# The weighted sum of an eight-head graph attention in three stretches in place of four, with the copy of its result a slot earlier

## Chip, cores, metric

One of the cores of a Trainium2 chip runs the whole kernel. The metric is the device time of one execution in microseconds (us), the median of several runs.

## What is computed

A stack of four graph layers over 8 batches of 1024 nodes with 64 features, each behind a layer norm and a ReLU, with a residual sum. The change concerns the fourth layer, an attention over the graph with 8 heads, followed by an attention with one head:

```
def gat_layer(x, graph, W, b):
    h = x @ W
    s = jnp.einsum('bnd,bmd->bnm', h, h) * graph
    s = jnp.where(s == 0.0, NEG_INF, s)
    a = jax.nn.softmax(s, axis=2)
    return jnp.einsum('bnm,bmd->bnd', a, h) + b
heads = jax.vmap(lambda W, b: gat_layer(flow_x, graph, W, b))(Wh, bh)
```

with 8 heads of 128 hidden features. A leaky ReLU and the second, single-head layer follow. The last sum of a head, weights times values, is what the change regroups.

## The kernel before, in words

`hidden_attention` (from line 335) does the 8 heads. A *unit* g is one head of one batch; there are 64, eight per batch. A unit has eight tiles of 128 rows by 1024 columns of scores. The scores are taken as x (W W^T) x^T, so a unit first needs y = (W W^T) x^T (`project`, L450 and L453), rounded and split into a high and a low part.

A tile goes through these steps:

- `score` (TensorE, L466): eight matmul records of 128x512 in two halves go into one of two PSUM buffers, `ps_score[i % 2]`. It waits until the mask of tile i-2 has read that buffer (`masked_ready`).
- `mask_tile` (VectorE, L559): mask and row minimum into a ring of four buffers in SBUF (the trace calls it x_sb). It waits for the scores.
- `exp_tile` (ScalarE, L627): the exponential in place, with the row sum.
- `turn_tile` (VectorE, L569): a transpose of 32x32 blocks into `weights_t`.

In the trace each score group has four matmuls (hi, lo, hi, lo) and one mask.

When all eight tiles of a unit are turned, `values` (TensorE, L484) computes the weighted sum: 32 key blocks of 32 rows, for each four matmuls, one for each group of 32 rows of the array, 256 columns wide, into four banks of `ps_low`. The trace shows eight records for a block. The 32 blocks are cut into four parts of 8 blocks, 64 records each. Then `copy_z` (ScalarE, L635) copies the sum z to SBUF, POOL divides it by the row sums (`normalise`, L694), `head_out` (TensorE, L496) multiplies it by the head's weights, `activate` (ScalarE, L642) adds the bias, `leaky` (VectorE, L574) is the leaky ReLU, and `project_out` (TensorE, L504) multiplies by wo. `take_out` (ScalarE, L651 or L654) copies the share and POOL adds it up (L705).

The order of each engine is written out by hand: a loop over g from 0 to 65, and in it over eight slots t. TensorE in slot t of unit g issues the scores of tile 8g+t+2; in slot 0 also `head_out(g-2)`; in slots 2 to 5 the four parts of `values(g-1)`; in slot 6 `project_out(g-2)`, which waits for `z_ready` of the sum just taken, since it writes one of its banks; in slot 7 `project(g+2)`. VectorE in slot t turns tile 8g+t-1 and masks tile 8g+t+2; in slot 1 it also inverts the row sums (L580), in slot 2 it does `leaky`. ScalarE in slot t does the exponential of tile 8g+t; in slot 0 also `copy_y` (L622) and `activate`, in slot 6 `copy_z` and `take_out`, in slot 7 `round_y` (L617). Part 0 of `values` waits for the last transpose of its unit and for `hidden_read`, which `activate` gives. Work queued behind a wait on the same engine waits too.

In the first two units of seven of the eight turns over the batches (g % 8 of 1 or 2, g under 56) the next batch's rows are transposed: `turn_rows` (TensorE, L443, 16 records, slot 6, behind `z_ready`), `round_rows` (ScalarE, L610), `split_rows` (VectorE, L551, slot 7), and the next `head_out` waits for that split (`x_split`).

SP stores the inverse row sums (L423) and loads them spread over the partitions (L427), and after g % 8 of 1 loads the next batch's rows in 16 transfers.

Of the kernel before, what the change touches and what calls it, by code (L numbers as in the profile page):

```python
# [334 lines left out]
def hidden_attention(nc, m, w, x_saved):  # L335

    name = "hid"
    UNITS = B * HEADS
    TILES = UNITS * NT
    Q = 32  # L340
    NB = N // Q
    RING = 4

    with ExitStack() as ctx:
# [52 lines left out]
        def wide(lo):  # L397
            return m.ps_low[:, lo:lo + 2, :].rearrange("p a n -> p (a n)")

        def y_banks(g):  # L400
            return 0 if g == 0 else 2

        def prep_bank(n, k):
            return k if n == 0 else 1
# [32 lines left out]
        def _(pe):  # L437
            def turn_rows(n, part):
                bank = prep_bank(n, part)
                for k in range(4):  # L440
                    t = 4 * part + k
                    for c in range(2):
                        ins = pe.matmul(m.ps_low[c * F:(c + 1) * F, bank, k * P:(k + 1) * P],  # L443
                                        m.h[:, t, n, :], m.ident[:], start=True, stop=True)
                ins.then_inc(x_turned, 1)
# [12 lines left out]
            def score(i):  # L458
                g, t = i // NT, i % NT
                if t == 0:  # L460
                    pe.wait_ge(y_split, g + 1)
                if i >= 2:
                    pe.wait_ge(masked_ready, i - 1)
                for half in range(2):
                    for k in range(2):
                        ins = pe.matmul(m.ps_score[:, i % 2, half * HALF:(half + 1) * HALF],  # L466
                                        xs[:, g // HEADS % 2, t * P:(t + 1) * P],
                                        y[g % 2][k][:, half * HALF:(half + 1) * HALF],
                                        start=(k == 0), stop=(k == 1))
                ins.then_inc(scores_ready, 1)  # L470

            def values(g, part):
                if part == 0:
                    if g % HEADS == 0:
                        pe.wait_ge(rows_loaded, 16 * 16 * (g // HEADS + 1))
                    pe.wait_ge(tile_turned, (g + 1) * NT)
                    if g:
                        pe.wait_ge(hidden_read, g)
                    if g + 2 < UNITS:
                        pe.wait_ge(y_copied, g + 3)  # L480
                for b in range(part * NB // 4, (part + 1) * NB // 4):
                    c = b % 2
                    for a in range(P // Q):
                        ins = pe.matmul(m.ps_low[c * F:(c + 1) * F, a, 0:NT * Q],  # L484
                                        x_rep[a * Q:(a + 1) * Q, g // HEADS % 2, b, :],
                                        weights_t[a * Q:(a + 1) * Q, g % 2, b, :, :],
                                        start=(b == c), stop=(b == NB - 2 + c))
                if part == 3:
                    ins.then_inc(values_ready, 1)

            def head_out(g):
                pe.wait_ge(z_normed, g + 1)
                if g:
                    pe.wait_ge(out_taken, g)
                for half in range(2):
                    ins = pe.matmul(m.ps_low[:, half, :], wz[:, g % HEADS, :],  # L496
                                    z[:, half * HALF:(half + 1) * HALF], start=True, stop=True)
                ins.then_inc(hidden_ready, 1)
# [24 lines left out]
            for g in range(UNITS + 2):  # L523
                n, u = g // HEADS + 1, g % HEADS
                for t in range(NT):
                    if g * NT + t + 2 < TILES:
                        score(g * NT + t + 2)
                    if t == 0 and g >= 2:
                        if n < B and u in (2, 3):
                            pe.wait_ge(x_split, 2 * n + u - 1)  # L530
                        head_out(g - 2)
                    if 2 <= t < 6 and 1 <= g <= UNITS:
                        values(g - 1, t - 2)
                    if t == 6 and n < B and u in (1, 2):
                        pe.wait_ge(z_ready, g)
                        turn_rows(n, u - 1)
                    if t == 6 and g >= 2:
                        project_out(g - 2)
                    if t == 7 and g + 2 < UNITS:
                        if g:  # L540
                            pe.wait_ge(z_ready, g)
                        else:
                            pe.wait_ge(y_copied, 2)
                        project(g + 2)
# [61 lines left out]
        @block.scalar  # L606
        def _(act):
            def round_rows(n, part):
                act.wait_ge(x_turned, 2 * n + part + 1)
                act.copy(xs[:, n % 2, part * HALF:(part + 1) * HALF],  # L610
                         m.ps_low[:, prep_bank(n, part), :]).then_inc(x_hi_ready, 1)

            def round_y(g):
                act.wait_ge(y_ready, g + 1)
                if g >= 2:
                    act.wait_ge(scores_ready, (g - 1) * NT)
                act.copy(y[g % 2][0][:], wide(y_banks(g))).then_inc(y_hi, 1)  # L617

            def copy_y(g):
                if g:  # L620
                    act.wait_ge(y_split, g)
                act.copy(y_wide[:], wide(y_banks(g))).then_inc(y_copied, 1)  # L622

            def exp_tile(i):
                g, t = i // NT, i % NT
                act.wait_ge(masked_ready, i + 1)
                act.activation(ring[:, i % RING, :], ring[:, i % RING, :], ACT.Exp, scale=-1.0,  # L627
                               bias=neg_max[:, g % 2, t:t + 1],
                               accum_out=row_sum[:, g % 2, t:t + 1]).then_inc(exp_ready, 1)

            def copy_z(g):
                act.wait_ge(values_ready, g + 1)
                if g:
                    act.wait_ge(hidden_ready, g)
                act.copy(z[:].rearrange("p (t a j) -> p a t j", t=NT, a=P // Q),  # L635
                         m.ps_low[:, :, 0:NT * Q].rearrange("p a (t j) -> p a t j", j=Q)).then_inc(z_ready, 1)

            def activate(g):
                act.wait_ge(hidden_ready, g + 1)
                if g:  # L640
                    act.wait_ge(out_ready, g)
                act.activation(hidden[:], wide(0), ACT.Identity, bias=bias[:, g % HEADS:g % HEADS + 1])\  # L642
                   .then_inc(hidden_read, 1)

            def take_out(g):
                act.wait_ge(out_ready, g + 1)
                adds = g - (g + HEADS - 1) // HEADS
                if adds > 0:
                    act.wait_ge(out_added, adds)
                if g % HEADS == 0:  # L650
                    act.copy(m.h[:, :, g // HEADS, :], m.ps_low[:, 0, :].rearrange("p (t f) -> p t f", f=F))\  # L651
                        .then_inc(out_taken, 1)
                else:
                    act.copy(share[:], m.ps_low[:, 0, :]).then_inc(out_taken, 1)  # L654

            round_rows(0, 0)
            round_rows(0, 1)
            for h in range(HEADS):
                act.wait_ge(gram_ready, h + 1)
                act.copy(gram[0][:, h, :], m.ps_low[:, h % 2, 0:P]).then_inc(gram_hi, 1)  # L660
            round_y(0)
            copy_y(0)
            round_y(1)
            for g in range(UNITS + 2):
                n, u = g // HEADS + 1, g % HEADS
                for t in range(NT):
                    if g < UNITS:
                        exp_tile(g * NT + t)
                    if t == 0 and g + 1 < UNITS:
                        copy_y(g + 1)  # L670
                    if t == 0 and g >= 2:
                        activate(g - 2)
                    if t == 6 and 1 <= g <= UNITS:
                        copy_z(g - 1)
                    if t == 6 and g >= 2:
                        take_out(g - 2)
                    if t == 6 and n < B and u in (1, 2):
                        round_rows(n, u - 1)
                    if t == 7 and g + 2 < UNITS:
                        round_y(g + 2)  # L680
# [1491 lines left out]
```

## Time and profile before

| | |
|---|---|
| median of 3 runs | 2644.24 us (2639.65 to 2645.26) |
| the profiled execution | 2645.69 us, its span 2644.0 us |
| TensorE matmul / VectorE busy | 2193.0 / 2202.7 us, 83% each |
| ScalarE / POOL busy | 1466.0 / 601.4 us, 55% / 23% |
| mean granted clock of TensorE | 0.914 of full speed |
| the eight-head attention's weighted sums | first record at 1038.0, last at 2336.6 us |

The profile comes from one profiled execution. Its page gives busy times and the costliest groups of instructions; further views give the busy time of a stretch of the span and the timeline of single instructions. In the timeline a row is start, duration, engine, line, operation, output and inputs, shape and count; a note in brackets is the idle time of that engine just before and what ended it. PE is TensorE's matmul, PEld its weight load, DVE is VectorE, ACT ScalarE, SPq the SyncE queue. Matmuls overlap, so starts tell more than durations.

### The profile page before, as it was taken

The numbers are of one execution on the slowest core, as the hardware profiler recorded it, in microseconds if no ns is written. First come the engines' busy times: TensorE is split into PE (matmuls) and PEld (weight loads), VectorE is DVE, ScalarE is ACT, GpSimd is POOL, SyncE is SP. The second block draws the span as 40 slices with busy tenths as digits, with TensorE's granted clock in tenths as the row PEclk, the third lists the DMA queues.
The fourth block names the chain that finished last, engine by engine and source line by source line (L and its number), as shares of the span: only waits on it lengthen the run. The fifth ranks groups of instructions, "written<-read, shape, count | busy, mean of one in ns | idle before, by whom it ended". The sixth has DMA issues, their size and how long they took to land. (4 is left out here: it accounts for less than half of the span.)

```text
span 2644.0 us, 57816 instructions
## 1 busy us (share of the span) xinstructions
PE 2193.0 (83%) x24398; PEld 1475.3 (56%) x24398; DVE 2202.7 (83%) x2944; ACT 1466.0 (55%) x2331; POOL 601.4 (23%) x354
## 2 busy tenths in 40 slices
PE   3855555837775957999999999999999999968997
PEld 2633324525454745666666666666666666646665
DVE  6558896478886447999999999999999999947775
ACT  2412221239984205666676666766667666737664
POOL 0026664000000001332332323323333233310000
PEclk8967887968987967999999999999999999989999
DMA  3000000000000003111001010010100100010000
GB/s 110 1 0 0 0 0 0 1 1 1 1 1 2 1 3 73 42 34 42 26 26 49 27 42 26 26 50 27 42 26 26 50 26 26 26 49 1 1 1 33
DMA packets 61879, 60.79 MB, mean 23 GB/s; under 512 B 50368, under 2 KB 51520, under 8 KB 60992
## 3 DMA queue, kind: packets, MB, share of 16 engines
q1 hardware_dynamic: 61632, 57.21, 7.1%
q8 instruction: 190, 3.11, 0.5%
q14 instruction: 57, 0.47, 0.1%
HBM read 44.34 MB, written 4.46 MB: 18 GB/s over the span
## 5 line engine op out<-in xcount | busy, mean ns | idle before, releaser
L627 ACT ACTIVATE x_sb<-x_sb,hid_neg_max 128x1024 f32<-128x1024 f32 x512 | 586.9, 1151 | 236.9 <-DVE hid_neg_max L559 236.7
L559 DVE CUSTOM_DVE_ANT_0 x_sb<-ps_score,adj_mask,row_scale 128x1024 f32<-128x1024 f32 x512 | 639.9, 1250 | 15.2 <-PE ps_score L466 14.8
L569 DVE STREAM_TRANSPOSE hid_weights_t<-x_sb 128x1024 f32<-128x1024 f32 x512 | 635.2, 1241 | 12.8 <-ACT x_sb L627 11.5
L484 PE MATMUL ps_low<-hid_weights_t,hid_x_rep 32*64 32x256 f32 x16384 | 506.7, 380 | 1.3 <-ACT hid_hidden L642 1.3
L466 PE MATMUL ps_score<-hid_y_hi,hid_xs 128*128 128x512 f32 x1024 | 464.8, 454 | 7.0 <-DVE hid_neg_max L559 4.8
L484 PEld LDWEIGHTS ps_low<-hid_weights_t,hid_x_rep 32*64 32x64 f32 x16384 | 345.9, 131 | 139.5 <-issue 88.2
L466 PE MATMUL ps_score<-hid_y_lo,hid_xs 128*128 128x512 f32 x1024 | 404.6, 395 | 0.0
L694 POOL TENSOR_TENSOR hid_z<-hid_z,hid_inv_cols 128x1024 f32<-128x1024 f32 x64 | 195.5, 3055 | 716.7 <-ACT hid_z L635 716.7
L466 PEld LDWEIGHTS ps_score<-hid_y_hi,hid_xs 128*128 128x128 f32 x1024 | 193.0, 189 | 202.5 <-issue 151.6
L466 PEld LDWEIGHTS ps_score<-hid_y_lo,hid_xs 128*128 128x128 f32 x1024 | 194.2, 190 | 42.4 <-issue 14.8
L687 POOL TENSOR_TENSOR hid_y_lo<-hid_y_wide,hid_y_hi 128x1024 fp32r<-128x1024 f32 x64 | 153.4, 2397 | 239.4 <-ACT hid_y_wide L622 239.4
L1785 ACT ACTIVATE hyp_blend_exp<-hyp_blend,hyp_minus_one 128x512 f32<-128x512 f32 x72 | 52.0, 723 | 161.8 <-DVE hyp_blend L1848 161.8
L168 PE MATMUL ps_low<-ident,gat_weights 128*128 128x128 f32 x512 | 79.9, 307 | 61.8 <-ACT gat_weights_t L257 55.7
L496 PE MATMUL ps_low<-hid_z,hid_wz 128*128 128x512 f32 x256 | 123.3, 605 | 3.5 <-POOL hid_z L694 3.5
L168 PEld LDWEIGHTS ps_low<-ident,gat_weights 128*128 128x128 f32 x512 | 64.1, 157 | 86.0 <-issue 43.3
L220 DVE CUSTOM_DVE_ANT_0 out_masked<-ps_score,out_mask 128x1024 f32<-128x1024 f32 x64 | 78.4, 1224 | 27.7 <-issue 22.2
L250 ACT ACTIVATE out_weights<-out_masked,out_neg_max 128x1024 f32<-128x1024 f32 x64 | 73.5, 1149 | 46.6 <-DVE out_neg_max L220 46.0
L627 ACT ACTIVATION_READ_ACCUMULATOR x_sb<-x_sb,hid_neg_max 128x1 f32 x512 | 98.3, 192 | 0.0
L1802 POOL TENSOR_TENSOR hyp_share<-hyp_share,hyp_pool_coef 128x512 f32<-128x512 f32 x72 | 78.4, 1089 | 82.7 <-DVE hyp_share L1858 82.7
L635 ACT COPY hid_z<-ps_low 128x1024 f32<-128x1024 f32 x64 | 65.1, 1018 | 57.2 <-PE ps_low L484 57.2
L1805 POOL TENSOR_TENSOR h_sb<-h_sb,hyp_share 128x512 f32<-128x512 f32 x72 | 93.9, 1303 | 5.6
L1858 DVE SCALAR_TENSOR_TENSOR hyp_share<-hyp_blend_exp,hyp_blend 128x512 f32<-128x512 f32 x72 | 83.7, 1171 | 12.2 <-DVE hyp_blend L1848 12.2
(308 smaller groups left out, 3708.3 us busy)
## 6 DMA issues: line engine op xcount, KB each, us to landing
hid_inv_cols<-hid_inv_rows SPq DMA_DIRECT2D x64, 512.0 KB, 3.7
hid_x_rep<-h_sb SPq DMA_DIRECT2D x128, 64.0 KB, 2.6
adj_rows<-in_adj SPq DMA_DIRECT2D x8, 512.0 KB, 7.6
x_sb<-in_x SPq DMA_DIRECT2D x2, 1024.0 KB, 6.2
x_saved<-x_sb SPq DMA_DIRECT2D x1, 2048.0 KB, 8.6
x_sb<-x_saved SPq DMA_DIRECT2D x1, 2048.0 KB, 8.1
out_x<-x_sb SPq DMA_DIRECT2D x1, 2048.0 KB, 7.2
hid_inv_rows<-hid_row_inv SPq DMA_DIRECT2D x64, 4.0 KB, 1.4
```

The lines of the kernel that those rows point to most:

```text
L168: ins = pe.transpose(m.ps_turn[:, half, k * P:(k + 1) * P], a.weights[:, t % 3, j * P:(j + 1) * P], m.ident[:])
L220: dve.tensor_tensor_reduce(a.masked[:, t % 2, :], scores, mask, -1.0, HUGE, ALU.add, ALU.min, a.neg_max[:, par, t:t + 1]).then_inc(a.maske ...
L466: ins = pe.matmul(m.ps_score[:, i % 2, half * HALF:(half + 1) * HALF], xs[:, g // HEADS % 2, t * P:(t + 1) * P], y[g % 2][k][:, half * HAL ...
L484: ins = pe.matmul(m.ps_low[c * F:(c + 1) * F, a, 0:NT * Q], x_rep[a * Q:(a + 1) * Q, g // HEADS % 2, b, :], weights_t[a * Q:(a + 1) * Q, g ...
L496: ins = pe.matmul(m.ps_low[:, half, :], wz[:, g % HEADS, :], z[:, half * HALF:(half + 1) * HALF], start=True, stop=True)
L559: dve.tensor_tensor_reduce(ring[:, i % RING, :], m.ps_score[:, i % 2, :], m.mask[:, t, :], m.row_scale[:, t, g // HEADS:g // HEADS + 1], HUGE,
L569: dve.transpose(weights_t[:, g % 2, :, t, :], ring[:, i % RING, :].rearrange("p (b j) -> p b j", j=Q)).then_inc(tile_turned, 1)
L627: act.activation(ring[:, i % RING, :], ring[:, i % RING, :], ACT.Exp, scale=-1.0, bias=neg_max[:, g % 2, t:t + 1], accum_out=row_sum[:, g ...
L687: pool.tensor_tensor(y[g % 2][1][:], y_wide[:], y[g % 2][0][:], ALU.subtract)\
L694: pool.tensor_tensor(rows, rows, inv_cols[:].rearrange("p i t -> p t i"), ALU.mult)\
L1805: pool.tensor_tensor(rows[:, t, :], rows[:, t, :], s, ALU.add)\
L1858: dve.scalar_tensor_tensor(out=s, in0=blend_exp[:, t % 2, :], scalar=1.0, in1=blend[:, t % 2, :], op0=ALU.min, op1=ALU.max).then_inc(share ...
```

## The change

`values` cuts the 32 key blocks into three parts, of 10, 11 and 11 blocks, in slots 2 to 4. The last part signals `values_ready`, as before. ScalarE's `copy_z` moves from slot 6 to slot 5, where it stands behind the exponential of slot 5 and ahead of that of slot 6. Nothing else is changed: `project_out` stays in slot 6.

```
-                for b in range(part * NB // 4, (part + 1) * NB // 4):
+                for b in range(part * NB // 3, (part + 1) * NB // 3):
...
-                if part == 3:
+                if part == 2:
                     ins.then_inc(values_ready, 1)
...
-                    if 2 <= t < 6 and 1 <= g <= UNITS:
+                    if 2 <= t < 5 and 1 <= g <= UNITS:
                         values(g - 1, t - 2)
...
-                    if t == 6 and 1 <= g <= UNITS:
+                    if t == 5 and 1 <= g <= UNITS:
                         copy_z(g - 1)
                     if t == 6 and g >= 2:
                         take_out(g - 2)
```

## Rows read from the trace of the kernel before

**Rows 1.** The page: busy time of the engines, and two groups

```profile
PE 2193.0 (83%) x24398; PEld 1475.3 (56%) x24398; DVE 2202.7 (83%) x2944; ACT 1466.0 (55%) x2331; POOL 601.4 (23%) x354
...
L484 PE MATMUL ps_low<-hid_weights_t,hid_x_rep 32*64 32x256 f32 x16384 | 506.7, 380 | 1.3 <-ACT hid_hidden L642 1.3
...
L694 POOL TENSOR_TENSOR hid_z<-hid_z,hid_inv_cols 128x1024 f32<-128x1024 f32 x64 | 195.5, 3055 | 716.7 <-ACT hid_z L635 716.7
```

**Rows 2.** Busy time in one plain unit, from copy of z to copy of z

```profile
1605.19:1625.55 20.36, 20.21 (x303) 13.12 (x304) 20.10 (x27) 13.93 (x21) 6.75 (x3) 1.00 0.08 28
```

**Rows 3.** Timeline of TensorE in that unit

```profile
1614.36 1.98 PE L484 MATMUL ps_low<-hid_weights_t,hid_x_rep 32*64 32x256 f32 x64
...
1623.46 1.98 PE L484 MATMUL ps_low<-hid_weights_t,hid_x_rep 32*64 32x256 f32 x64
...
1625.38 0.50 PE L466 MATMUL ps_score<-hid_y_hi,hid_xs 128*128 128x512 f32 x1
...
1626.71 1.08 PE L504 MATMUL ps_low<-hid_hidden,hid_wo 128*64 128x512 f32 x4
```

**Rows 4.** Timeline of the other engines there, in order of time

```profile
1624.53 1.25 DVE L559 CUSTOM_DVE_ANT_0 x_sb<-ps_score,adj_mask,row_scale 128x1024 f32<-128x1024 f32 x1
...
1625.55 1.02 ACT L635 COPY hid_z<-ps_low 128x1024 f32<-128x1024 f32 x1 [0.83 <-PE ps_low L484]
...
1631.53 1.24 DVE L559 CUSTOM_DVE_ANT_0 x_sb<-ps_score,adj_mask,row_scale 128x1024 f32<-128x1024 f32 x1
...
1635.58 1.25 DVE L569 STREAM_TRANSPOSE hid_weights_t<-x_sb 128x1024 f32<-128x1024 f32 x1 [0.26 <-ACT x_sb L627]
```

**Rows 5.** Timeline of the last two units' stretches, and the copies of z

```profile
2320.41 1.98 PE L484 MATMUL ps_low<-hid_weights_t,hid_x_rep 32*64 32x256 f32 x64
...
2322.50 1.01 ACT L635 COPY hid_z<-ps_low 128x1024 f32<-128x1024 f32 x1 [0.57 <-PE ps_low L484]
...
2329.78 7.17 PE L484 MATMUL ps_low<-hid_weights_t,hid_x_rep 32*64 32x256 f32 x256 [1.30 <-ACT hid_hidden L642]
```

**Rows 6.** Timeline of the first unit: v0, and a mask that waits

```profile
1038.01 1.98 PE L484 MATMUL ps_low<-hid_weights_t,hid_x_rep 32*64 32x256 f32 x64
...
1049.02 0.50 PE L466 MATMUL ps_score<-hid_y_hi,hid_xs 128*128 128x512 f32 x1
...
1050.25 1.28 DVE L559 CUSTOM_DVE_ANT_0 x_sb<-ps_score,adj_mask,row_scale 128x1024 f32<-128x1024 f32 x1 [0.52 <-PE ps_score L466]
...
1052.62 1.24 DVE L559 CUSTOM_DVE_ANT_0 x_sb<-ps_score,adj_mask,row_scale 128x1024 f32<-128x1024 f32 x1
...
1054.66 1.98 PE L496 MATMUL ps_low<-hid_z,hid_wz 128*128 128x512 f32 x4
...
1055.91 1.28 DVE L559 CUSTOM_DVE_ANT_0 x_sb<-ps_score,adj_mask,row_scale 128x1024 f32<-128x1024 f32 x1
```

**Rows 7.** Timeline: scores that wait for a mask, with a stretch behind

```profile
2291.68 1.98 PE L484 MATMUL ps_low<-hid_weights_t,hid_x_rep 32*64 32x256 f32 x64
...
2308.85 1.25 DVE L559 CUSTOM_DVE_ANT_0 x_sb<-ps_score,adj_mask,row_scale 128x1024 f32<-128x1024 f32 x1
...
2310.16 0.19 PEld L466 LDWEIGHTS ps_score<-hid_y_hi,hid_xs 128*128 128x128 f32 x1 [0.56 <-DVE hid_neg_max L559]
...
2311.29 1.98 PE L484 MATMUL ps_low<-hid_weights_t,hid_x_rep 32*64 32x256 f32 x64
```

**Rows 8.** Timeline of a unit with rows of the next batch

```profile
1707.01 1.02 ACT L635 COPY hid_z<-ps_low 128x1024 f32<-128x1024 f32 x1 [0.84 <-PE ps_low L484]
...
1713.30 1.95 PE L496 MATMUL ps_low<-hid_z,hid_wz 128*128 128x512 f32 x4
...
1717.07 1.98 PE L484 MATMUL ps_low<-hid_weights_t,hid_x_rep 32*64 32x256 f32 x64
...
1728.28 1.02 ACT L635 COPY hid_z<-ps_low 128x1024 f32<-128x1024 f32 x1 [0.63 <-PE ps_low L484]
```

**Rows 9.** Busy time near the end of the stage, with the clock

```profile
2310.00:2329.00 19.00, 15.33 (x281) 8.97 (x280) 16.60 (x23) 10.66 (x18) 4.08 (x2) 1.00 0.10 30
```

## The prediction

> **What bounds the kernel now.** I began with the page [rows 1]: TensorE and VectorE are both busy for 83% of the span, and the diff is all in the eight-head attention. The busy time of one unit of it (one head of one batch) [rows 2] shows TensorE busy for 20.21 and VectorE for 20.10 of 20.36 us, at the full granted clock. The shares can't say which of the two paces the unit, so I followed the timeline round one unit. I call s_t and m_t the scores and the mask that TensorE and VectorE reach in slot t (tile 8g+t+2 of unit g), and v0, v1, ... the stretches of the weighted sum.
>
> TensorE [rows 3]: v0 starts at 1614.36, each further stretch 3.03 later (v3 at 1623.46), s6 at 1625.38. The product with wo, queued behind s6, comes at 1626.71, right behind the copy of z, which started at 1625.55 and took 1.02 [rows 4]. Behind scores that follow a stretch the next work otherwise starts after 1.12 (a slot of 3.03 less the 1.92 of its stretch, 1623.46 to 1625.38); here it took 1.33, so 0.21 is a stall for the copy, TensorE's one in the unit. VectorE [rows 4] is idle once, 0.26 before the transpose at 1635.58, behind an exponential that was late because the head product was. So TensorE's order plus the copy of z is the loop that closes in 20.36 us; VectorE alone would need 20.10.
>
> **What the change removes.** A switch between scores and a stretch. A slot with a stretch takes 3.035; four scores matmuls take 0.93. The stretch's own rate: 64 records took 1.98 and 256 took 7.17 [rows 5], so 5.19 / 192 = 27.0 ns each, 1.73 for 64. The rest, 3.035 - 0.93 - 1.73 = 0.37, is the switch there and back, once less per unit. And the copy of z, now in ScalarE's slot 5, is over before s6 is: the 0.21 go too. TensorE alone would need 20.36 - 0.37 - 0.21 = 19.78 us. The trace shows what a switch costs; the Trainium skill (TensorEngine Tiling (Array Packing), Key Properties) says that a change of tiling mode drains TensorE, so by that rule alone one change less is a gain.
>
> **What it lengthens.** Blocks go 10, 11, 11, so stretches have 80, 88 and 88 records. From a 64-record stretch to the scores behind it is 1.915 (a fourth of 11.02 less three times 1.12, v0 to s6 [rows 3]), so now 2.35, 2.56, 2.56; from such scores to the next stretch 1.12. Two stretches longer by 0.65 each now stand ahead of s5, and scores have only two PSUM buffers, so masks can't draw on a deeper stock. From v0 to s5: 2.35 + 1.12 + 2.56 + 1.12 + 2.56 = 9.71; before, s5 was at 3 x 1.915 + 2 x 1.12 = 7.99.
>
> **The new loop**, link by link:
> - s5 to m5, when the mask waits: 1049.02 to 1050.25 [rows 6], 1.23. A mask that has waited is followed by the next one, with a transpose between, after 2.37 (1052.62), where three such steps take 7.00 below, 2.33 each: 0.04 more.
> - m5 to the next unit's m0: 1624.53 to 1631.53 [rows 4], 7.00, plus that 0.04: 7.04.
> - m0 to s2 and v0: s2 overwrites the buffer that m0 reads, and v0 is queued behind s2. TensorE's own order would bring s2 to that wait 0.5 early. What it then costs is seen in the one unit where TensorE has less to do [rows 7]: mask 2308.85, scores 2310.16, stretch 2311.29. So 1.31, then 1.13.
> - v0 to s5: 9.71.
>
> Sum 1.23 + 7.04 + 1.31 + 1.13 + 9.71 = 20.42 us, against 20.36. **Both engines then wait in every unit**: VectorE about 0.3 for s5 (its own m0 to m5 is 20.10 - 7.00 = 13.10, where TensorE takes 1.31 + 1.13 + 9.71 + 1.23 = 13.38), TensorE about 0.5 for m0 ahead of s2. The stall is not removed, it goes to these two places.
>
> **Work beside it, costed at nothing.** Exponential 6 stands behind the copy of z on ScalarE. The copy starts 0.17 after s5's start and ends 1.19 after it, the exponential some 1.1 later: 1.05 after m5, where its transpose is wanted 3.5 after m5. If that cover were gone, VectorE would wait by the excess. The take-out of the shares waits for the wo product as before, SP's loads of the next rows wait for the stretches' end, which comes sooner. POOL's normalisation waits for z and for the inverse sums that SP spreads; all its idle time is put down to z, 716.7 us before 64 of them [rows 1], and at worst the sums would let it start where it did, which was early enough. Nothing moves past SP's or POOL's queues.
>
> **Units with rows of the next batch** (14 of them) have 16 transposing matmuls behind s6, VectorE's split in slot 7 and a head product that waits for the split. Now the copy-of-z stall stands in their loop too, which takes 21.26 us, as from 1707.01 to 1728.28 [rows 8]. After the change: v0 to s5 9.71, to m5 1.23, to m7 4.71 (2 x 2.335 + 0.04), to the head product 2.04 (mask 1052.62 to product 1054.66 [rows 6], the split between them), to the next v0 3.77 (1713.30 to 1717.07 [rows 8]): 21.46. The very first such unit took 20.42 (1038.01 to 1054.66, and 3.77 [rows 6]) as VectorE had a lead; that lead is spent on s5.
>
> **The end.** The unit that starts at 2291.68 issues no projection and took 19.61 to the next v0 at 2311.29 [rows 7]; VectorE's loop doesn't depend on that projection: 20.42 now. In the last but one, v0 to the copy of z was 11.21 (2311.29 to 2322.50 [rows 5, 7]) with the head product, the bias and the last stretch in series behind it; it becomes 7.15 to the start of the third stretch (9.71 less 2.56) + 2.09 (2320.41 to 2322.50) + 0.65 = 9.89: a gain of 1.32.
>
> **Sum.** 47 plain units x 0.06 = +2.8; 13 units with rows x 0.20 = +2.6; the first +1.04; the one without projection +0.81; the end -1.32. In all **+5.9 us**. The profiled execution took 2645.69 (span 2644.0 and 1.69 around it), 1.45 above the median of 2644.24. So 2651.6 against the former, about 2650 against the latter.
>
> Bounds. The rate of added records: 25.5 ns if they go as the first 64 (1.98 less the 0.38 of the last one [rows 1], over 63), or 29.9 if the whole 1.915 grows with the count; I take 27.0, the only rate measured beyond 64 records. 64 records are added ahead of s5: -0.10 to +0.19 us per unit, -6 to +12 over 62 units. The 0.04 of a waiting mask may be nothing: -2.5. The upper end speaks against the 256 records, so I keep half of it: this case spans about 2642 to 2656.
>
> **Rivals.**
> A. VectorE stays fed (faster; 12%). Were s5 ready when m5 is due, a plain unit would close at VectorE's 20.10: 47 x 0.26 = 12.2. A unit with rows needs 0.95 more of VectorE (mask 1052.62 to mask 1055.91 [rows 6] is 3.29 in place of 2.34), 21.05: 13 x 0.21 = 2.7. With 1.3 at the end that is 16.2, 2628. It decides from the point where v0 to m5 is under 13.10 - 2.44 = 10.66 us; I have 10.94. Against it: no row has a stretch that cheap. The Trainium skill (Perfetto Trace Analysis, Identifying Performance Opportunities) advises in general to improve the most-contended engine; by occupancy that is TensorE here, and this rival is what its 0.59 less work would give at most.
> B. The links are there but at their cheap end (no change; 15%): added records at 25.5 ns and a waiting mask at no extra price make the plain unit 20.28, a unit with rows 21.32: -3.8 + 0.8 + 0.9 + 0.7 - 1.4 = -2.8, 2641. For it: within a stretch the first 64 records do go faster.
> C. The granted clock falls, as TensorE gets two more pauses (3%). At the lower level the 7.7 us of stretches in a unit would double; ten such units are 77 us, 2720. Against it: from 2310 to 2329 TensorE is busy for 15.3 of 19 us and the clock is 1.00 [rows 9].
> The copy of z may fail to come as early as I say; its 0.21 would then lie within TensorE's new pause ahead of s2, so the plain unit stays at 20.42, and this takes no chance of its own.
>
> **Numbers.** A measurement of this kernel tells about 0.2%, 5.3 us, from no change, and +5.9 is hardly beyond it. The forecast has 70%: 46 for slower, 24 for the same. A's 12 are faster; of B's 15, 9 are the same and 6 faster; C's 3 are slower. Faster 0.18, same 0.33, slower 0.49. The range 2637 to 2657 holds the forecast's bounds and B with a little below it, and leaves out A and C.
>
> **What would show it.** Plain units of 20.42 between copies of z; a VectorE idle of about 0.3 ahead of m5 put down to the scores, once per unit, and none of 0.26 behind the exponential; TensorE idle ahead of s2 put down to the mask; stretches of 80 and 88 records of about 2.4 and 2.6 us; no wait of the wo product for z. Units of 20.1 would speak for A, of 20.3 for B; an idle of VectorE in another place would mean that I missed a link.

## The result, and the profile after

The changed kernel takes 2673.78 us (median of 4 runs, 2673.08 to 2675.51) beside 2644.75 for the one before: a ratio of 1.0115, interval 1.0097 to 1.0132. That is 29 us slower, where 6 slower was forecast with a range up to 2657. The profiled execution took 2673.33, its span 2671.6.

The time lies in the units of the eight-head attention. First a copy of z in the timeline of ScalarE, then three groups on the page of the kernel before (busy, mean ns, idle before and its releaser), then the same groups and the weighted sum on the page of the changed kernel:

```profile
1615.28 1.01 ACT L635 COPY hid_z<-ps_low 128x1024 f32<-128x1024 f32 x1 [1.91 <-PE ps_low L484]
```

```profile
L559 DVE CUSTOM_DVE_ANT_0 x_sb<-ps_score,adj_mask,row_scale 128x1024 f32<-128x1024 f32 x512 | 639.9, 1250 | 15.2 <-PE ps_score L466 14.8
L569 DVE STREAM_TRANSPOSE hid_weights_t<-x_sb 128x1024 f32<-128x1024 f32 x512 | 635.2, 1241 | 12.8 <-ACT x_sb L627 11.5
L466 PE MATMUL ps_score<-hid_y_hi,hid_xs 128*128 128x512 f32 x1024 | 464.8, 454 | 7.0 <-DVE hid_neg_max L559 4.8
```

```profile
L559 DVE CUSTOM_DVE_ANT_0 x_sb<-ps_score,adj_mask,row_scale 128x1024 f32<-128x1024 f32 x512 | 640.1, 1250 | 62.5 <-PE ps_score L466 62.1
L569 DVE STREAM_TRANSPOSE hid_weights_t<-x_sb 128x1024 f32<-128x1024 f32 x512 | 632.2, 1235 | 0.4
L484 PE MATMUL ps_low<-hid_weights_t,hid_x_rep 32*64 32x256 f32 x16384 | 514.6, 379 | 1.3 <-ACT hid_hidden L642 1.3
L466 PE MATMUL ps_score<-hid_y_hi,hid_xs 128*128 128x512 f32 x1024 | 462.6, 452 | 27.2 <-DVE hid_neg_max L559 25.2
```

The next copy starts at 1636.08: a plain unit takes 20.80 us, not 20.36 [rows 2] and not the 20.42 of the forecast; the 47 plain units average 20.80 after and 20.36 before. The idle time of VectorE behind the exponential is gone (0.4 us ahead of all transposes, where it was 12.8), as was forecast, and 62.1 us ahead of the masks, put down to the scores, stand in place of 14.8. TensorE has 25.2 us ahead of its scores put down to the masks, in place of 4.8. Both waits of the forecast are there. How they lie in one unit, in the timeline:

```profile
1602.63 1.24 DVE L559 CUSTOM_DVE_ANT_0 x_sb<-ps_score,adj_mask,row_scale 128x1024 f32<-128x1024 f32 x1
...
1603.94 0.50 PE L466 MATMUL ps_score<-hid_y_hi,hid_xs 128*128 128x512 f32 x1 [0.38 <-DVE hid_neg_max L559]
...
1605.05 2.41 PE L484 MATMUL ps_low<-hid_weights_t,hid_x_rep 32*64 32x256 f32 x80
...
1607.40 0.50 PE L466 MATMUL ps_score<-hid_y_hi,hid_xs 128*128 128x512 f32 x1
...
1608.53 2.82 PE L484 MATMUL ps_low<-hid_weights_t,hid_x_rep 32*64 32x256 f32 x88
...
1611.28 0.50 PE L466 MATMUL ps_score<-hid_y_hi,hid_xs 128*128 128x512 f32 x1
...
1612.40 2.82 PE L484 MATMUL ps_low<-hid_weights_t,hid_x_rep 32*64 32x256 f32 x88
...
1615.15 0.50 PE L466 MATMUL ps_score<-hid_y_hi,hid_xs 128*128 128x512 f32 x1
...
1616.38 1.28 DVE L559 CUSTOM_DVE_ANT_0 x_sb<-ps_score,adj_mask,row_scale 128x1024 f32<-128x1024 f32 x1 [0.79 <-PE ps_score L466]
...
1623.42 1.24 DVE L559 CUSTOM_DVE_ANT_0 x_sb<-ps_score,adj_mask,row_scale 128x1024 f32<-128x1024 f32 x1
```

Read as the forecast's links: m0 to s2 1.31 (1602.63 to 1603.94; forecast 1.31), s2 to v0 1.11 (1.13), v0 to s3 2.35 (2.35), then v1 to s4 and v2 to s5 2.75 each, where 2.56 was forecast; s5 to m5 1.23 (1.23), m5 to the next m0 7.04 (7.04). One kind of link is off, twice: 2 x 0.19 = 0.38, and 20.42 + 0.38 = 20.80. A stretch of 80 records lasts 2.41 and one of 88 lasts 2.82, so the last eight records cost 0.41, nearly as much as sixteen do from 64 (1.98 [rows 5]) to 80.

### The profile page after: what moved, and what is told of

The parts are those of the page before. It is cut to its first block and busy times, and to the rows that moved or that the text cites. A ratio compares the mean times of both kernels' runs of the same rounds, so it can differ in the third digit from the quotient of the medians.

```text
span 2671.6 us, 57816 instructions
## 1 busy us (share of the span) xinstructions
PE 2202.2 (82%) x24398; PEld 1499.2 (56%) x24398; DVE 2198.3 (82%) x2944; ACT 1461.3 (55%) x2331; POOL 600.2 (22%) x354
## 5 line engine op out<-in xcount | busy, mean ns | idle before, releaser
L559 DVE CUSTOM_DVE_ANT_0 x_sb<-ps_score,adj_mask,row_scale 128x1024 f32<-128x1024 f32 x512 | 640.1, 1250 | 62.5 <-PE ps_score L466 62.1
L484 PE MATMUL ps_low<-hid_weights_t,hid_x_rep 32*64 32x256 f32 x16384 | 514.6, 379 | 1.3 <-ACT hid_hidden L642 1.3
L466 PE MATMUL ps_score<-hid_y_hi,hid_xs 128*128 128x512 f32 x1024 | 462.6, 452 | 27.2 <-DVE hid_neg_max L559 25.2
L484 PEld LDWEIGHTS ps_low<-hid_weights_t,hid_x_rep 32*64 32x64 f32 x16384 | 371.1, 131 | 128.0 <-issue 51.4
L466 PEld LDWEIGHTS ps_score<-hid_y_lo,hid_xs 128*128 128x128 f32 x1024 | 193.9, 189 | 43.0 <-issue 14.8
L220 DVE CUSTOM_DVE_ANT_0 out_masked<-ps_score,out_mask 128x1024 f32<-128x1024 f32 x64 | 78.4, 1225 | 27.5 <-issue 21.2
```

The costliest lines, as they stand in the source:

```text
L220: dve.tensor_tensor_reduce(a.masked[:, t % 2, :], scores, mask, -1.0, HUGE, ALU.add, ALU.min, a.neg_max[:, par, t:t + 1]).then_inc(a.maske ...
L484: ins = pe.matmul(m.ps_low[c * F:(c + 1) * F, a, 0:NT * Q], x_rep[a * Q:(a + 1) * Q, g // HEADS % 2, b, :], weights_t[a * Q:(a + 1) * Q, g ...
L559: dve.tensor_tensor_reduce(ring[:, i % RING, :], m.ps_score[:, i % 2, :], m.mask[:, t, :], m.row_scale[:, t, g // HEADS:g // HEADS + 1], HUGE,
```

## The experiments

### Is it the odd count, or the length? Even counts, 10, 12, 10

```
-                for b in range(part * NB // 3, (part + 1) * NB // 3):
+                for b in range((0, 10, 22)[part], (10, 22, 32)[part]):
```

> Three stretches as in the changed kernel, but of 10, 12 and 10 key blocks in place of 10, 11 and 11. In the changed kernel a stretch of 80 records is followed by scores after 2.35 us, one of 88 records after 2.75, where 2.56 was forecast, and plain units take 20.80 us, not 20.42. Theory P (pairs): even and odd blocks write different column halves of the array and run at the same time, so a pair of blocks takes 0.43 us and a block left alone takes 0.43 as well; a stretch with an odd count pays for half a pair that isn't there. It expects 96 records to be followed by scores after 2.78 us (2.35 + 0.43), v0 to s5 in 9.72, plain units of 20.42, and 2650 us in all, 23 less than the changed kernel. Theory L (length): records beyond 80 in one stretch cost 50 ns each, whatever their parity. It expects 3.16 us behind 96 records, units of 20.8 as now, and about 2673.

Measured: 2653.82 us, ratio to the kernel before 1.0039 (1.0023 to 1.0054), about 20 us less than the changed kernel. A unit in its timeline:

```profile
1619.50 2.41 PE L484 MATMUL ps_low<-hid_weights_t,hid_x_rep 32*64 32x256 f32 x80
...
1622.98 2.85 PE L484 MATMUL ps_low<-hid_weights_t,hid_x_rep 32*64 32x256 f32 x96
...
1625.76 0.50 PE L466 MATMUL ps_score<-hid_y_hi,hid_xs 128*128 128x512 f32 x1
...
1629.23 0.50 PE L466 MATMUL ps_score<-hid_y_hi,hid_xs 128*128 128x512 f32 x1
...
1630.48 1.28 DVE L559 CUSTOM_DVE_ANT_0 x_sb<-ps_score,adj_mask,row_scale 128x1024 f32<-128x1024 f32 x1 [0.47 <-PE ps_score L466]
```

96 records last 2.85, hardly more than the 2.82 of 88, and the scores behind them come after 2.78. The length theory (3.16) falls. Plain units are 20.45 (20.42 expected), v0 to s5 is 9.73. With even counts, then, the prediction's loop gives the plain unit within 0.03. The whole is not as close: 11 us above the kernel before by the medians, where 6 were forecast. In the traces, first stretch to last copy of z, it is 9.3 us more (1299.03 to 1308.36); the units with rows of the next batch average 21.57, not 21.46, and a few of them stand out (one of 22.41), which is not explained.

### The same with four short stretches, 7, 9, 7, 9

```
-                for b in range(part * NB // 4, (part + 1) * NB // 4):
+                for b in range((0, 7, 16, 23)[part], (7, 16, 23, 32)[part]):
```

> The kernel before, with its four stretches of 7, 9, 7 and 9 key blocks in place of 8 each: nothing beyond 72 records in a stretch, the same number of switches. Theory P: 7 blocks take as long as 8 and 9 as long as 10, so two stretches cost 0.43 us more, v0 to s6 is 11.88 in place of 11.02, plain units 21.2 us, and some 52 us more in all, 2697. Theory L expects no change, 2645 and units of 20.36.

Measured: 2687.43 us, ratio 1.017 (1.015 to 1.019). Timeline of TensorE:

```profile
1612.14 1.96 PE L484 MATMUL ps_low<-hid_weights_t,hid_x_rep 32*64 32x256 f32 x56
...
1615.15 2.39 PE L484 MATMUL ps_low<-hid_weights_t,hid_x_rep 32*64 32x256 f32 x72
```

7 blocks last as long as 8 (1.96 and 1.98), 9 as long as 10 (2.39 and 2.41), though no stretch has 80 records. Plain units take 21.09 us and the whole is some 45 us longer, where 21.2 and 52 were expected: an odd stretch is 0.03 cheaper than the even one above it, not equal to it.

### Neighbours on the same column half

Blocks alternate between two column halves of the array by their parity (`c = b % 2`). Here each stretch does its even blocks first:

```
-                for b in range(part * NB // 4, (part + 1) * NB // 4):
+                for b in (8 * part + k for k in (0, 2, 4, 6, 1, 3, 5, 7)):
```

> The kernel before with its four stretches of 8 blocks, but in each the four even blocks first and then the four odd ones, so that neighbours write the same column half. Theory P (even and odd blocks run at the same time on the two column halves; a block by itself takes the 0.43 us of a pair): hardly a block has a partner of the other half beside it, so a stretch takes 7 or 8 times 0.43 us, 3.0 to 3.4, in place of 1.7; plain units 25.5 to 27 us and 320 to 430 us more in all, 2965 to 3075. If only the count of blocks in a stretch matters (an uneven remainder, not the halves), nothing changes: 2643.

Measured: 2873.5 us, ratio 1.0858 (1.083 to 1.0886): 228 us more, plain units of 23.99. A stretch of the same 64 records lasts 2.90 in place of 1.98. So it is not the mere remainder: the order of the halves counts. The size was expected too high (a stretch of 3.0 to 3.4, 320 to 430 us in all). What overlaps shows in the count of weighted-sum records in flight (begun and not yet ended by the profile) within windows of 0.1 us of one stretch. The rows give the window, its length, TensorE's busy time, (xrecords), clock and DMA. First the kernel before, stretch from 1623.46, beside the changed one, stretch of 88 from 1612.40:

```profile
1624.00:1624.10 0.10, 0.10 (x16) 1.00 0.00 0
1624.50:1624.60 0.10, 0.10 (x17) 1.00 0.00 0
1625.20:1625.30 0.10, 0.10 (x13) 1.00 0.00 0
```

```profile
1613.40:1613.50 0.10, 0.10 (x16) 1.00 0.00 0
1614.80:1614.90 0.10, 0.10 (x10) 1.00 0.00 0
1615.00:1615.10 0.10, 0.10 (x4) 1.00 0.00 0
```

And the version with one half after the other, stretch from 1623.62:

```profile
1624.10:1624.20 0.10, 0.10 (x8) 1.00 0.52 205
1624.40:1624.50 0.10, 0.10 (x8) 1.00 0.80 328
1625.00:1625.10 0.10, 0.10 (x17) 1.00 1.08 287
1625.80:1625.90 0.10, 0.10 (x8) 1.00 0.31 123
```

Alternating blocks keep 16 records or more in flight, blocks of one half only 8. In the changed kernel the count is already down to 10 some 0.4 us before the end of an odd stretch and to 4 some 0.2 before it, where the last block is alone; in the even stretch of the kernel before it is still 13 at the latter distance. In the other version the count is above 8 from 1624.50 to 1625.70, with 17 in the row shown, where the last even blocks run beside the first odd ones: more than the one pair that I had allowed for, which would explain why it cost less than expected; no run tests that. Transfers run during this stretch (the last two columns), but the stretches around it last 2.90 too. The Trainium skill (TensorEngine Tiling (Array Packing), Key Properties) says that tiles work independently, weight loads and matmuls of different tiles in parallel; these counts agree, and show what the parallel half is worth: at least 0.92 us on a stretch of 1.98, as some overlap is left in the 2.90.

### The copy of z back in slot 6

The even version above, and:

```
-                    if t == 5 and 1 <= g <= UNITS:
+                    if t == 6 and 1 <= g <= UNITS:
                         copy_z(g - 1)
```

> As e1_even_three, but the copy of z stays in slot 6 behind exponential 6, as in the kernel before: the other half of the change undone. By the loop of the prediction (m0 to s2 to v0 to s5 to m5 to m0) the copy is not in the loop in either place, TensorE pauses for 0.5 us ahead of s2 anyway: the same time as e1_even_three within 1 us (plain units 20.42). A rival, that the earlier copy brings its 0.21 us per unit, expects e1_even_three to be 13 us faster than this one.

Measured: 2654.16 us, ratio 1.0045 (1.003 to 1.006), beside 2653.82 and 1.0039 with the copy in slot 5; plain units 20.46 beside 20.45. With the stretches in slots 2 to 4 the place of the copy makes no difference.

### The place of the third stretch: slots 2, 3, 5

Even counts, the copy of z in slot 6 as in the kernel before, and against the changed kernel:

```
-                    if 2 <= t < 5 and 1 <= g <= UNITS:
-                        values(g - 1, t - 2)
+                    if t in (2, 3, 5) and 1 <= g <= UNITS:
+                        values(g - 1, (2, 3, 5).index(t))
```

> A version meant to beat both kernels: three stretches of 10, 12 and 10 blocks in slots 2, 3 and 5, the copy of z in slot 6 as before. One switch less, but only two stretches ahead of s5. The loop theory: v0 to s5 is 2.35 + 1.12 + 2.78 + 1.03 = 7.3 us, well under the 10.66 at which VectorE begins to wait; v0 to s6 is 7.3 + 1.01 + 2.35 = 10.64, so TensorE with the stall for the copy needs 19.98 us a unit and VectorE its 20.10. Plain units of 20.10, 2628 us in all. If fewer stretches are dear by themselves (a rival that blames the three stretches and not their place), plain units stay at 20.4 or above and the time at 2650.

Measured: 2624.22 us, ratio 0.9931 (0.9917 to 0.9944), faster than both kernels. The busy time of a plain unit (columns as in [rows 2]):

```profile
1594.41:1614.40 19.99, 19.85 (x303) 13.36 (x304) 19.99 (x27) 13.93 (x21) 6.74 (x3) 1.00 0.09 29
```

Three stretches were never the trouble; three ahead of s5 were. The unit is even shorter than the 20.10 that I took for VectorE's own need. VectorE is busy for all of the 19.99 us, and it is tempting to say that it paces the unit. The versions with the wo product in slot 7, below, show that it doesn't: TensorE's order with the wait for the copy of z does, which the expectation had at 19.98.

### Slots 2, 4, 5

```
-                    if t in (2, 3, 5) and 1 <= g <= UNITS:
-                        values(g - 1, (2, 3, 5).index(t))
+                    if t in (2, 4, 5) and 1 <= g <= UNITS:
+                        values(g - 1, (2, 4, 5).index(t))
```

> As the version in slots 2, 3 and 5 but in slots 2, 4 and 5: again two stretches ahead of s5 and one behind. The loop theory counts only how much weighted sum stands between s2 and s5 (7.3 us in either): the same time, 2624 within 2 us, plain units of 19.99. The rival that two scores groups in a row after v1 helped in that version would expect a few us more here.

Measured: 2629.27 us, ratio 0.9933 (0.9911 to 0.9955), beside 0.9931 for slots 2, 3, 5; the interval is some 12 us wide and can't tell the same time from a few us more. The traces can. Plain units are 20.06, 0.07 above, and units with rows 21.15, 0.27 above; from the first copy of z to the last it is 1274.0 us beside 1266.8. So the rival's few us more are there and the expected 19.99 failed. A scores group behind v0 now waits for a mask, as in this row of its timeline, which is a link that I had not counted:

```profile
1628.54 0.19 PEld L466 LDWEIGHTS ps_score<-hid_y_hi,hid_xs 128*128 128x128 f32 x1 [0.23 <-DVE hid_neg_max L559]
```

### The odd counts in slots 2, 3, 5

The changed kernel's 10, 11 and 11 in slots 2, 3 and 5, with the copy in slot 6.

> The changed kernel's stretches of 10, 11 and 11 blocks, with the odd remainders, in slots 2, 3 and 5, the copy of z in slot 6: the place changed and the sizes not. An odd stretch costs 0.20 more than its share, 0.40 for two (0.37 against 10, 12 and 10 by the rows). TensorE's order with the copy then needs 19.99 + 0.38 = 20.37 and paces: plain units of 20.37, 2643, no change against the kernel before, 30 us less than the changed kernel. If the odd remainder only hurts where a mask waits for s5, plain units stay at 19.99 and the time at 2624.

Measured: 2640.05 us, ratio 0.9986 (0.9976 to 0.9996), plain units 20.32 (20.37 expected). The odd blocks cost 0.33 us here too, though masks wait for scores no longer than before (14.1 us in all beside 14.8), and eat up most of what the place brings.

### What closed the loop in the kernel before

The kernel before, with the wo product and the take-out in slot 7:

```
-                    if t == 6 and g >= 2:
+                    if t == 7 and g >= 2:
                         project_out(g - 2)
...
-                    if t == 6 and g >= 2:
-                        take_out(g - 2)
...
+                    if t == 7 and g >= 2:
+                        take_out(g - 2)
```

> The kernel before, four stretches of 8, with only the wo product moved from slot 6 to slot 7, behind s7, and the take-out of the share with it: the copy of z then has a whole group of scores more to finish. If the loop of before is TensorE's order plus the wait for the copy, the 0.21 us of that wait go: plain units of 20.15, 47 x 0.21 = 10 us less, 2633 (the longer units keep their wait, of the transposing matmuls). If something else closed the loop at 20.36 (VectorE's 20.10 with its idle 0.26), nothing moves: 2643.

Measured: 2637.95 us, ratio 0.9969 (0.9957 to 0.9981). Plain units 20.13 (20.15 expected): the wait for the copy of z was the stall that counted. The units with rows of the next batch grew from 21.24 to 21.50 on average and gave 3 us back, and the end of the stage gave back 1.7 (below, at the last version). Moving the stall away changed the time, so TensorE's order plus that wait did close the loop; VectorE's idle 0.26 did not.

### Both, everywhere and only in plain units

> The version with stretches of 10, 12 and 10 in slots 2, 3 and 5, and the wo product and the take-out in slot 7 as well. TensorE alone would then need 19.78 us a unit. In the version without this VectorE was busy for 19.99 of 19.99 us. So the theory that VectorE now paces expects nothing: plain units of 19.97 to 19.99, 2624 within 2 us. The rival that TensorE's order with the copy of z (20.36 - 0.37 = 19.99) still paces expects 19.8 and some 10 us less, 2614.

Measured: 2621.05 us, ratio 0.9902 (0.9881 to 0.9922); units with rows 21.13. The first two plain units behind those take 19.74 to 19.82, as TensorE alone would (19.78), the others 19.86 to 19.92; the average is 19.86. The theory that VectorE already paced at 19.99 falls: taking TensorE's wait away shortened the unit. The rival was right on what paced, but didn't see that VectorE's own need comes next, just below. That need shows in the steps between masks. First slots 2, 3, 5 without the late wo product, then this version:

```profile
1623.11 1.24 DVE L559 CUSTOM_DVE_ANT_0 x_sb<-ps_score,adj_mask,row_scale 128x1024 f32<-128x1024 f32 x1
...
1625.59 1.24 DVE L559 CUSTOM_DVE_ANT_0 x_sb<-ps_score,adj_mask,row_scale 128x1024 f32<-128x1024 f32 x1
```

```profile
1603.77 1.24 DVE L559 CUSTOM_DVE_ANT_0 x_sb<-ps_score,adj_mask,row_scale 128x1024 f32<-128x1024 f32 x1
...
1621.25 1.24 DVE L559 CUSTOM_DVE_ANT_0 x_sb<-ps_score,adj_mask,row_scale 128x1024 f32<-128x1024 f32 x1
...
1623.66 1.24 DVE L559 CUSTOM_DVE_ANT_0 x_sb<-ps_score,adj_mask,row_scale 128x1024 f32<-128x1024 f32 x1
```

The step with the inverse of the row sums in it takes 2.48 in the first and 2.41 in the second, and neither row has a note of idle time: VectorE can lose a little to a wait and still count as busy throughout. A unit of the second is 19.89 (1603.77 to 1623.66). The last version keeps the wo product early in the units with rows:

```
-                    if t == 7 and g >= 2:
+                    if t == (6 if n < B and u in (1, 2) else 7) and g >= 2:
                         project_out(g - 2)
```

and the same for `take_out`, ahead of `round_rows`.

> As e7_both, but in the units with rows of the next batch the wo product and the take-out stay in slot 6. In e7_both plain units take 19.88 us and those 21.13, in e5_slots_2_3_5 19.99 and 20.87. If the two places act on their own unit alone, this takes the better of each: 13 x 0.26 = 3.4 us less than e7_both, some 2618 beside 2645 for the kernel before. The rival, that a unit's gain is only handed on to the next, expects no change against e7_both.

Measured: 2617.88 us, ratio 0.9896 (0.988 to 0.9913). Units with rows are back at about 20.87, plain ones take 19.89. From the first copy of z to the last the traces have 1264.6 us beside 1266.4 for the version before it, about half of the 3.4 expected, as plain units are 0.04 longer; the two ratios' intervals overlap. Busy time of one unit:

```profile
1327.77:1347.64 19.87, 19.87 (x303) 13.24 (x304) 19.87 (x27) 13.93 (x21) 6.74 (x3) 1.00 0.10 29
```

TensorE and VectorE are both busy for all of it. It has the lowest time of this study, 27 us under the kernel before and some 56 under the changed one, though the version before it is not clearly slower.

The last weighted sum tells of one thing more. First the head product ahead of it and the granted clock (the third number from the end of its rows) in the kernel before, then in the last version, with the sum itself:

```profile
2326.50 1.98 PE L496 MATMUL ps_low<-hid_z,hid_wz 128*128 128x512 f32 x4 [1.77 <-POOL hid_z L694]
2326.50:2329.50 3.00, 1.98 (x4) 1.00 0.03 1
```

```profile
2296.21 3.78 PE L496 MATMUL ps_low<-hid_z,hid_wz 128*128 128x512 f32 x4 [1.79 <-POOL hid_z L694]
2296.00:2301.00 5.00, 3.78 (x4) 0.50 0.34 103
2301.29 9.08 PE L484 MATMUL ps_low<-hid_weights_t,hid_x_rep 32*64 32x256 f32 x256 [1.29 <-ACT hid_hidden L642]
```

The granted clock is 1.00 in every unit up to there (2.4 GHz) and 0.50 (1.2 GHz) in this stretch. The head product takes 3.78 in place of 1.98, and the 256 records 9.08 in place of 7.17 [rows 5]. The last two copies of z are 18.29 apart, in place of 14.54. TensorE was busy for 1.08 of the 4 us ahead of the head product in both, at 1.00 before and at 0.85 on average in the last version, so these rows don't say what makes the difference. Every version with even counts in slots 2, 3, 5 or 2, 4, 5, or with the late wo product, has this fall at the end (15.99 apart in slots 2, 3, 5; 16.23 in the version with only the late wo product), the changed kernel and the one with odd counts in slots 2, 3, 5 don't (14.55 in both). Without the fall the last version would be 3.75 us shorter, an estimate from these two distances.

## Why the prediction was right or wrong

- **The direction and the mechanism were right.** The stall went from the copy of z to s5 and to the mask ahead of s2; the rows after show both, and with even counts the loop of the prediction comes out at 20.45 against 20.42. The size was not: +29 us in place of +6.
- **The step that failed** is the term "the stretch's own rate ... 27.0 ns each", used in "so now 2.35, 2.56, 2.56". It was taken between 64 and 256 records, both whole numbers of pairs, and applied to 88, which is five pairs and a half. By the starts of the scores behind it a pair costs 0.43 us; its first block costs 0.40 of that and the second 0.03. Two odd stretches add 2 x 0.19 = 0.38 us to every unit, 62 x 0.38 = 23.6 us. With it the forecast's sum is 5.9 + 23.6 = 29.5, where the medians differ by 29.0. The traces have v0 of the first unit to the last stretch as 1038.01 to 2329.78 before [rows 5, 6] and 1035.17 to 2357.09 after, 30.15 us more; the stage began 2.84 us earlier in the changed kernel's profiled execution, so the span grew by only 27.6.
- **The bounds missed it for the same reason.** They varied the rate from 25.5 to 29.9 ns, as if records were a fluid. My upper end, half of +12 us, had no room for a remainder. That the eight blocks of a stretch alternate between two halves stands in the kernel's own code (`c = b % 2`), and the trace could have been asked what the last one costs.
- **The first unit** was forecast at 21.46 and took 21.85, 1035.17 to 1057.02; the units with rows 21.46 and 21.83; the one without projection 20.42 and 20.80; each is off by 0.37 to 0.39. The end was forecast at 1.32 less and took 17.53 (2339.56 to 2357.09) in place of 18.49, 0.96 less, again by 0.38.
- **"The 0.21 go too"** was right and without worth in this place: the copy moved or not, the time is the same, as the last paragraph of the rivals said. That the 0.21 closed the loop of the kernel before is shown by the version with only the wo product moved (20.13).
- **"VectorE alone would need 20.10"** was too high. It works through a unit in 19.88 when nothing makes it wait. The 20.10 is the unit less the noted idle of 0.26, and a wait costs more than its note. In the kernel before, two steps from mask to mask around that wait take 5.22 us, in the last version 4.74:

```profile
1611.17 1.25 DVE L559 CUSTOM_DVE_ANT_0 x_sb<-ps_score,adj_mask,row_scale 128x1024 f32<-128x1024 f32 x1
...
1616.39 1.24 DVE L559 CUSTOM_DVE_ANT_0 x_sb<-ps_score,adj_mask,row_scale 128x1024 f32<-128x1024 f32 x1
```

```profile
1334.30 1.24 DVE L559 CUSTOM_DVE_ANT_0 x_sb<-ps_score,adj_mask,row_scale 128x1024 f32<-128x1024 f32 x1
...
1339.04 1.24 DVE L559 CUSTOM_DVE_ANT_0 x_sb<-ps_score,adj_mask,row_scale 128x1024 f32<-128x1024 f32 x1
```

That is 0.48 more, and 20.36 - 0.48 = 19.88. The 20.10 sized rival A at 2628, and the idle of "about 0.3" ahead of m5, which was 0.47 with even counts and 0.79 in the changed kernel; it didn't enter the sum.

- **Slips that changed nothing.** The text ahead of the prediction gives a scores group eight matmul records in one place; the trace has four, and the 0.93 counts four. TensorE's wait for m0 is 20.42 - 19.78 = 0.64 by the prediction's own terms, not "about 0.5"; the note in the trace is 0.38. The "0.59 less work" of rival A is 0.37 + 0.21 = 0.58, and 0.21 of it is a wait, not work. TensorE is the busier engine only within a unit (20.21 against 20.10); over the span VectorE is (2202.7 against 2193.0 [rows 1]).
- **Rival A** was wrong for this change. With one stretch behind s5 its condition, v0 to m5 under 10.66 us, is met and the time is 2624, near its 2628. That nearness is luck: what paced there was TensorE's order with the wait for the copy, at 19.99, which rival A took as gone, and not VectorE at 20.10.
- **Rival C** didn't happen in the changed kernel: the granted clock is 1.00 in its units and at the end of the stage, with two pauses in each unit. It is 1.00 in the units of every other version too, but falls to 0.50 ahead of the last weighted sum in five of them, as shown above.

## What to carry to other kernels

With two buffers between two engines, what counts is not how much work the faster one saves in a round but how much of it stands in one piece between two things that the other one needs; split work goes where a need is not due. When small matmuls alternate over parts of the array, cut them only at whole rounds of those parts, and take the cost of a size from rows at that size or at the step below and above it, not from a rate. An engine that counts as busy throughout doesn't pace for that reason: move the suspected wait of the other engine and see whether the time moves. And look at the end of a stage as well as at its middle, since a gain in each unit can be followed by a slower end.

## What the runs showed of the hardware

- Blocks of four row groups on the two column halves: stretches of 7, 8, 9, 10, 11 and 12 blocks last 1.96, 1.98, 2.39, 2.41, 2.82 and 2.85 us. An odd block costs 0.41, its partner 0.02 to 0.03.
- All blocks of one half in a row: 8 records in flight in place of 16 for most of the stretch, 2.90 us in place of 1.98 for 64.
- A switch from scores to a stretch and back cost 0.37 by the estimate; with one less the even version in slots 2, 3, 5 gives 19.99 where 20.36 - 0.37 = 19.99 was worked out.
- The granted clock fell from 1.00 to 0.50 ahead of the last weighted sum in five versions; there the head product takes up to 3.78 us in place of 1.98. The kernel before has as long a pause there and stays at 1.00; the cause is open.
- Why the pair takes 0.43 and a run of one half about 0.3 a block is not settled; whether weight loads or the shared rows limit it wasn't tried.
